# An attention and expert layer on one core: score units in pairs, triangles cleared by Pool, q and k split from the banks, first q sent in parts

## The chip, the cores and the metric

The kernel runs on one core of a Trainium2 chip. The metric is the device time of one execution in microseconds, lower is better. The core has TensorE (PE, its weight loads shown as PEld), VectorE (DVE), ScalarE (ACT), GpSimd (Pool) and SyncE (SP); SP, ACT and Pool issue the transfers.

## What is computed

The input has 4 batches of 512 tokens with 128 channels. Attention has 16 heads of 8 channels, a linear bias over the key position, and a causal mask; behind it stands a layer of 8 experts of which the best one's gate scales the sum of all outputs.

```python
q, k, v = (layernorm(x) @ w_attn + b_attn).reshape(b, t, 3, H, D).transpose(2, 0, 3, 1, 4)
scores = einsum('bhtd,bhsd->bhts', q, k) / sqrt(D) + slopes[None, :, None, None] * pos[None, None, None, :]
attn = softmax(where(causal, scores, -inf), axis=-1)
x = x + einsum('bhts,bhsd->bhtd', attn, v).transpose(0, 2, 1, 3).reshape(b, t, c) @ w_proj + b_proj
logits = layernorm(x) @ gate_w.T + gate_b            # normalised, softmax, top 1
h = gelu(einsum('nd,edh->neh', layernorm(x), w1) + b1)
out = x + ((einsum('neh,ehd->ned', h, w2) + b2) * norm_g[:, None, None]).sum(axis=1)
```

## The kernel before, in words

A batch b is worked in four sets s of four heads, so there are 16 sets, n = 4b + s. The scores are computed twice. First come 11 max units of a set (`max_unit`, L748): queries on the partitions, into one of three banks `v_ring`, and DVE takes row maxima of each 128-wide query block from there (L1099). PE transposes the maxima (`transpose_max`, L755), DVE splits them into m_hi and m_lo (L1115, L1116), and SP sends these into rows of `q_stack` (`load_max`, L398), so that the second computation of the scores subtracts them by itself. Its 12 score units (`exp_unit` on PE, L768 with the mask product L774) have keys on the partitions, go into three banks `a_ring`, and ACT takes the exponential into `probs` (L571). There are three kinds: four of kind 0 hold key block 0 with 512 query columns and one 128-wide triangle to mask, four of kind 1 hold blocks 1 and 3 (384 and 128 columns, two triangles), four of kind 2 hold block 2 (256 columns, one triangle). The triangles are masked by adding -1e30 with a bf16 product of identity and `score_mask`. `pv` (L793) multiplies probabilities and v, a kind at a time.

q and k of a batch are projected, DVE adds the bias (and scales q) into `q_full` and `k_full` (`take_q` L1056, `take_k` L1071), ACT copies the high part in a shorter format (`split_high`, L612), Pool subtracts it for the low part (`split_low`, L457; for the first q it is DVE, L1063), and SP, ACT and Pool send the parts into `q_stack` (L379, three transfers of 256 KB for all four sets) and `k_stack` (L335, 32 KB each).

Each engine's order is written out by hand: a set has 16 places, and the tables EARLY_PLAN (sets 0 to 4) and LATER_PLAN say at which place of set n the units of the next set's maxima (-1 means the end of the set before), `take_max` and the transposed maxima, the set's own score units and its `pv` stand. STAGES puts the side work of other batches there (the projections, norms, gates). The expert layer of batch b-1 fills sets from 5 on, and the last one's runs as a tail from about 268 us. On each engine at a place: side work, max units, take_max, score units, pv. Pool does norms (`z_rstd`, `x_rstd`, `norm_logits`), its part of k's sends, and `residual`, set by set. In the first set five max units of set 1 stand ahead of the first score unit.

## Time and profile before

| | |
|---|---|
| time, median of 3 runs (lowest to highest) | 317.34 us (316.98 to 338.38) |
| the profiled execution's own time | 317.27 us |
| its span | 315.5 us |
| PE busy | 292.7 us, 93% |
| DVE busy | 204.4 us, 65% |
| ACT busy | 193.5 us, 61% |
| Pool busy | 85.7 us, 27% |

The profile is of one execution. The span is the time from the first to the last recorded instruction. Matmuls are pipelined and their ends are modelled, so that a matmul's duration is longer than the distance to the next one. An idle time is put down to the instruction or transfer that released the engine.

### The profile page before, as it was taken

To read this page: it belongs to the slowest core of one execution; us is meant where nothing else is said; L and a number is where in the kernel's file an instruction comes from. 1 tells how busy PE (TensorE), PEld (TensorE's weight loads), DVE (VectorE), ACT (ScalarE), POOL (GpSimd) and SP (SyncE) were. 2 spreads that over 40 slices of the span, in tenths; PEclk is the share of its full clock that TensorE was granted. 3 is DMA by queue.
4 is the path that set the end of the run, shared out by engine and by line. 5 is a ranking of instruction groups with operands and counts; after the bars stand their busy time and mean duration, and the time that the engine had idled before them with its cause. 6 is when DMAs were issued, how large, how long until landed. Compare 5 with 4: busy or idle time off the path is not lost.

```text
span 315.5 us, 5489 instructions
## 1 busy us (share of the span) xinstructions
PE 292.7 (93%) x1750; PEld 184.2 (58%) x1751; DVE 204.4 (65%) x817; ACT 193.5 (61%) x323; POOL 85.7 (27%) x213
## 2 busy tenths in 40 slices
PE   7658698999969999999999999999999999999993
PEld 2524355666636666657666666657666665657871
DVE  5528589788877768554777785556776821266871
ACT  6462255557447478758667396857487877535462
POOL 3349411521133065002321172020300501600250
PEclk9795599999999999999999999999999999999999
DMA  6254400130400013002200132002001000000101
GB/s 173 105 150 126 137 2 0 35 124 6 108 12 0 0 38 127 3 0 59 63 3 2 34 89 76 0 21 66 0 6 35 2 2 2 0 0 1 35 0 33
DMA packets 12524, 13.23 MB, mean 42 GB/s; under 512 B 2064, under 2 KB 9104, under 8 KB 12240
## 3 DMA queue, kind: packets, MB, share of 16 engines
q1 hardware_dynamic: 11376, 11.70, 12.0%
q0 software_dynamic: 1024, 1.05, 1.6%
q8 instruction: 14, 0.23, 0.3%
q10 hardware_dynamic: 96, 0.13, 0.2%
q14 instruction: 14, 0.11, 0.1%
HBM read 5.14 MB, written 1.05 MB: 20 GB/s over the span
## 4 chain that ended last, share of the span: by engine, by line
PE 76%; DVE 10%; POOL 4%; DMA 3%; issue 2%; ACT 1%; SPq 1%; DVEq 0%; POOLq 0%; ACTq 0%
PE ffn_bank L861 14%; PE pv_bank L793 11%; PE a_ring L768 11%; PE v_ring L748 11%; PE a_ring L697 5%; PE a_ring L774 5%; PE a_ring L699 4%; PE a_ring L698 4%; DVE unused L1099 4%; DMA q_stack<-q_lo 1%; DMA q_stack<-m_lo 1%; PE v_ring L755 1%; PE v_ring L697 1%; PE v_ring L806 1%; PE v_ring L698 1%
## 5 line engine op out<-in xcount | busy, mean ns | idle before, releaser
L1099 DVE CUSTOM_DVE_ANT_0 unused<-v_ring,cst 128x256 bf16<-128x256 f32 (+3 forms) x256 | 112.2, 487 | 53.1 <-PE v_ring L748 49.3
L571 ACT ACTIVATE probs<-a_ring 128x512 f32<-128x512 f32 (+1 forms) x192 | 91.8, 526 | 62.3 <-PE a_ring L774 61.6
L748 PE MATMUL v_ring<-k_stack,q_stack 128*128 128x512 f32 (+1 forms) x176 | 84.1, 519 | 4.9 <-DMA q_stack<-q_lo 3.3
L768 PE MATMUL a_ring<-q_stack,k_stack 128*128 128x512 f32 (+3 forms) x256 | 73.5, 351 | 2.2 <-DMA q_stack<-m_lo 2.2
L588 ACT ACTIVATE hidden<-a_ring,cols_sb 128x512 f32<-128x512 f32 x64 | 43.4, 689 | 29.5 <-PE a_ring L699 29.2
L768 PEld LDWEIGHTS a_ring<-q_stack,k_stack 128*128 128x128 f32 x256 | 47.5, 195 | 14.9 <-issue 8.7
L861 PE MATMUL ffn_bank<-hidden,w_sb 128*128 128x512 f32 x100 | 51.9, 604 | 0.9 <-ACT hidden L588 0.9
L774 PE MATMUL a_ring<-score_mask,ident_bf 128*128 128x128 bf16 (+1 forms) x192 | 47.7, 250 | 0.0
L748 PEld LDWEIGHTS v_ring<-k_stack,q_stack 128*128 128x128 f32 x176 | 34.6, 205 | 21.6 <-issue 11.4
L793 PE MATMUL pv_bank<-probs,v_ones 128*32 128x256 f32 (+3 forms) x512 | 42.3, 440 | 0.0
L774 PEld LDWEIGHTS a_ring<-score_mask,ident_bf 128*128 128x128 bf16 x192 | 18.6, 97 | 25.4 <-issue 19.9
L335 POOL DMA_DIRECT2D k_stack<-k_lo x32 | 18.1, 569 | 54.3 <-PE a_ring L774 49.7
L697 PE MATMUL a_ring<-zT_hi,w_hi 128*128 128x512 f32 x64 | 28.2, 441 | 0.8 <-DVEq L998 0.8
L699 PE MATMUL a_ring<-zT_hi,w_lo 128*128 128x512 f32 x64 | 25.2, 394 | 0.0
L698 PE MATMUL a_ring<-zT_lo,w_hi 128*128 128x512 f32 x64 | 25.1, 392 | 0.0
L1099 DVE DVE_READ_ACCUMULATOR2_ANT row_max<- 128x1 f32 x256 | 21.3, 83 | 0.0
L861 PEld LDWEIGHTS ffn_bank<-hidden,w_sb 128*128 128x128 f32 x100 | 16.4, 193 | 3.8 <-ACT hidden L588 2.1
L793 PEld LDWEIGHTS pv_bank<-probs,v_ones 128*32 128x32 f32 x512 | 12.3, 109 | 10.7 <-issue 8.3
L697 PEld LDWEIGHTS a_ring<-zT_hi,w_hi 128*128 128x128 f32 x64 | 12.0, 188 | 9.1 <-issue 4.4
L588 ACT ACT_TABLE_LOAD x13 | 16.7, 1283 | 0.2
L571 ACT ACT_TABLE_LOAD x11 | 14.1, 1283 | 0.2
L341 POOL TENSOR_SCALAR var<-mv 128x4 f32<-128x4 f32 x6 | 1.1, 188 | 47.7 <-DVE mv L1006 47.7
(123 smaller groups left out, 346.5 us busy)
## 6 DMA issues: line engine op xcount, KB each, us to landing
q_stack<-q_hi SPq DMA_DIRECT2D x8, 256.0 KB
k_stack<-k_hi SPq DMA_DIRECT2D x60, 32.0 KB
x_in<-x SPq DMA_DIRECT2D x4, 256.0 KB, 3.4
hidden<-w SPq DMA_DIRECT2D x1, 1024.0 KB, 7.5
k_stack<-k_lo POOLq DMA_DIRECT2D x32, 32.0 KB, 2.1
q_stack<-q_lo SPq DMA_DIRECT2D x4, 256.0 KB
w_sb<-w SPq DMA_DIRECT2D x1, 1024.0 KB, 5.1
x_res<-x SPq DMA_DIRECT2D x4, 256.0 KB, 3.1
```

The source lines that it names most:

```text
L335: queue.dma_start(k_stack[ROW_Q * q + g::ROW_D, 2 * half:2 * half + 2, q, :].bitcast(F32), part[rows:rows + QR // 2, :].bitcast(F32)).then ...
L571: act.activation(probs[:, n % 2, q, KIND_AT[kind]:KIND_AT[kind] + cols], a_bank()[:, 0:cols], ACT.Exp).then_inc(e_freed, 1)
L588: act.activation(hidden[:, n % HB, :], a_bank()[:], ACT.Gelu, bias=b1_cols[:, m:m + 1]).then_inc(g_freed, 1)
L697: pe.matmul(dst, lhs[0], rhs[0], start=True, stop=False)
L698: pe.matmul(dst, lhs[0], rhs[1], start=False, stop=False)
L699: return pe.matmul(dst, lhs[1], rhs[0], start=False, stop=True)
L748: pe.matmul(dst, q_stack[b % 2][:, s, n * P:(n + 1) * P], k_stack[:, s, quads[0]:quads[-1] + 1, 0:cols], start=True, stop=True).then_inc(v ...
L768: pe.matmul(dst[:, at:at + P * (TB - j)], k_stack[:, s, q, j * P:(j + 1) * P], q_stack[b % 2][:, s, j * P:T], start=(at == 0), stop=False, ...
L774: pe.matmul(diagonal, ident_bf[:], score_mask[:].unsqueeze(1).to_broadcast([P, blocks, P]), start=False, stop=True, skip_group_check=True) ...
L793: last = pe.matmul(pv_bank[QR * q:QR * (q + 1), j * P:T], v_ones[b % 2][:, j, s, q, :], probs[:, n % 2, q, at:at + cols], start=(s % 2 == ...
L861: pe.matmul(ffn_bank[:], w2_sb[:, m, :], hidden[:, n % HB, :], start=(m == 0), stop=(m == NT - 1)).then_inc(ffn2_done, 1)
L1099: ins = dve.tensor_tensor_reduce(unused[:, (uses[0] - 1) % V_BANKS, at:at + cols], bank_[:, at:at + cols], cst[:, C_MASK + T - cols:C_MASK ...
```

## The change

- The four kind-2 units become two units of two heads each (two products of 256 columns, one mask product over two triangles, one exponential of 512 columns): a set has 10 score units.
- Kind 0 has no mask product. A constant row of the score product puts -1e30 on the corner of keys 64 to 127 against queries 0 to 63, and Pool clears the whole triangle of all four heads in `probs` with one `affine_select` on 128x4x128 per set (`mask_probs`), which waits for the set's fourth exponential; `pv` of kind 0 waits for it. On Pool it stands in front of `norm_logits` and `z_rstd`.
- DVE splits q and k itself from the projection's bank, two operations a part; ACT's copies, Pool's subtractions and `q_full`, `k_full` are gone. The scale of q is multiplied into w_attn and its bias by Pool at the start, and the split of w_attn moves behind `xn_ready` there.
- The corner's constant (256 KB) is loaded fourth. The first batch's q goes out in twelve transfers of 64 KB, set 0's three first. m_lo of the first set is sent by ACT. w_proj, w2 and the residual are loaded behind set 1's maxima.
- Set 0 has a plan of its own (FIRST_PLAN) with six max units of set 1 ahead of it and the transposed maxima at place 6; the exponentials' places in the other plans are fitted to 10 units.

```diff
-    "exp": (4, 4, 5, 6, 8, 8, 9, 11, 11, 13, 14, 14), "pv": (11, 15), "pv_last": (0,),
+    "exp": (4, 4, 5, 6, 8, 8, 9, 11, 12, 14), "pv": (11, 15), "pv_last": (0,),
+FIRST_PLAN = {
+    "max": (-1, -1, -1, -1, -1, -1, 0, 1, 2, 3, 4), "take_max": (6,),
+    "exp": (0, 1, 2, 3, 4, 5, 6, 7, 9, 10), "pv": (9, 12), "pv_last": (0,),
+}
...
-    "exp": (4, 5, 6, 7, 8, 9, 10, 10, 12, 13, 14, 15), "pv": (12, 15), "pv_last": (0,),
+    "exp": (4, 5, 6, 7, 8, 9, 10, 10, 13, 15), "pv": (12, 15), "pv_last": (0,),
...
+    KIND_UNITS = [[(0,), (1,), (2,), (3,)], [(0,), (1,), (2,), (3,)], [(0, 1), (2, 3)]]
+    EXP_UNITS = [(kind, quads) for kind in range(KINDS) for quads in KIND_UNITS[kind]]
+    KIND_END = [4, 8, 10]
...
+            def load_first_q(s, loaded):
+                sp.wait_ge(q_const, SETS)
+                for g, part in ((0, 0), (1, 0), (2, 1)):
+                    sp.wait_ge(q_split, part + 1)
+                    sp.dma_start(q_stack[0][g::ROW_Q, s, :].bitcast(F32),
+                                 (q_hi, q_lo)[part][s::SETS, :].bitcast(F32)).then_inc(loaded, 16)
...
+            sp.dma_start(corner, consts[:, C_CORNER:]).then_inc(corner_loaded, 16)
...
             load_k(0, 0, [0])
-            load_q(0)
+            load_first_q(0, first_q_loaded)
             load_k(0, 0, [3])
+            for s in range(1, SETS):
+                load_first_q(s, q_loaded)
             load_k(0, 1)
-            sp.dma_start(w_proj_sb[:], w_proj).then_inc(wp_loaded, 16)
-            sp.dma_start(w2_sb[:], w2).then_inc(w2_loaded, 16)
-            load_residual(0)
+            load_max(0, 0)
             load_x(1)
-            load_max(0, 0)
...
+            def mask_probs(n):
+                pool.wait_ge(e_freed, UNITS * n + KIND_END[0])
+                triangle = probs[:, n % 2, :, 0:P]
+                pool.affine_select(out=triangle, in_=triangle, compare_op=ALU.is_ge, fill=0.0, base=0,
+                                   pattern=[[0, QUADS], [1, P]], channel_multiplier=-1).then_inc(probs_masked, 1)
...
+            pool.wait_ge(rows_loaded, 32)
             pool.wait_ge(wa_loaded, 16)
+            pool.wait_ge(xn_ready, 1)
+            settle(pool.tensor_scalar(w_attn_sb[:, 0:C], w_attn_sb[:, 0:C], float(D) ** -0.5, None, ALU.mult))
             split(w_attn_sb[:], w_attn_hi[:], w_attn_lo[:], wa_split, 0)
-            pool.wait_ge(xn_ready, 1)
...
+                    if s == 2 and b + 1 < B:
+                        load_k_low(b + 1, 0)
+                    mask_probs(SETS * b + s)
+                    if s == 2 and b >= 1:
+                        norm_logits(b - 1)
+                    if s == 0 and b >= 1:
+                        z_rstd(b - 1)
...
+                kind, quads = EXP_UNITS[k]
...
+                for q in quads:
+                    for j in KEY_BLOCKS[kind]:
+                        last = pe.matmul(dst[:, at:at + P * (TB - j)], k_stack[:, s, q, j * P:(j + 1) * P],
+                                         q_stack[b % 2][:, s, j * P:T], start=(at == 0), stop=(kind == 0),
...
+                if kind == 0:
+                    last.then_inc(e_filled, 1)
+                    return
...
-                pe.wait_ge(e_freed, UNITS * n + QUADS * (kind + 1))
+                if kind == 0:
+                    pe.wait_ge(probs_masked, n + 1)
+                else:
+                    pe.wait_ge(e_freed, UNITS * n + KIND_END[kind])
...
+            def split_biased(src, bias, hi, lo, parts):
+                settle(dve.tensor_scalar(hi[:], src, bias, None, ALU.add))
+                dve.sem_inc(parts, 1)
+                settle(dve.scalar_tensor_tensor(out=lo[:], in0=src, scalar=bias, in1=hi[:].bitcast(F32),
+                                                op0=ALU.add, op1=ALU.subtract))
...
+        c[corner, C_KEY + HALF:C_KEY + P] = MASKED_SCORE
+        c[corner, C_CORNER:C_CORNER + HALF] = 1.0
```

The order of instructions on SP at the start, from the first sends of k on (k_hi, q_hi and q_lo are the split parts, m_hi the high part of the maxima; the shape is partitions by elements). Before:

```order
L335 DMA k_stack<-k_hi 8x2x512 [waits k_split,k_const]
L335 DMA k_stack<-k_hi 8x2x512
L379 DMA q_stack<-q_hi 32x4x512 [waits q_split,q_const]
L379 DMA q_stack<-q_hi 32x4x512 [waits q_split]
L379 DMA q_stack<-q_lo 32x4x512 [waits q_split]
L335 DMA k_stack<-k_hi 8x2x512 [waits k_split,k_const]
L335 DMA k_stack<-k_hi 8x2x512
L335 DMA k_stack<-k_hi 8x2x512 [waits k_split,k_const]
L335 DMA k_stack<-k_hi 8x2x512 x7
L416 DMA w_proj_sb<-w_proj 128x128
L417 DMA w_sb<-w 128x2048
L367 DMA x_res<-x 128x4x128
```

After, the same stretch's first rows; eight more k transfers, m_hi and the load of x follow behind these:

```order
L344 DMA k_stack<-k_hi 8x2x512 [waits k_split,k_const]
L344 DMA k_stack<-k_hi 8x2x512
L401 DMA q_stack<-q_hi 32x512 [waits q_split,q_const]
L401 DMA q_stack<-q_hi 32x512 [waits q_split]
L401 DMA q_stack<-q_lo 32x512 [waits q_split]
L344 DMA k_stack<-k_hi 8x2x512 [waits k_split,k_const]
L344 DMA k_stack<-k_hi 8x2x512
L401 DMA q_stack<-q_hi 32x512 [waits q_split,q_const]
L401 DMA q_stack<-q_hi 32x512 [waits q_split]
L401 DMA q_stack<-q_lo 32x512 [waits q_split]
L401 DMA q_stack<-q_hi 32x512 [waits q_split,q_const]
L401 DMA q_stack<-q_hi 32x512 [waits q_split]
```

The three q transfers have a quarter of their size, nine more stand between them and the rest of k.

On Pool in set 6, from k's sends of the next batch to the start of the logits' norm (its first operation is the one on `mean_square`). Before:

```order
L335 DMA k_stack<-k_lo 8x2x512 [waits k_split,e_filled]
L335 DMA k_stack<-k_lo 8x2x512 x3
L341 TENSOR_SCALAR var<-mean_square 128x4 [waits square_ready]
L342 TENSOR_SCALAR inverse_rms<-var 128x4 [waits pool_step]
L349 TENSOR_TENSOR var<-inverse_rms 128x4 [waits pool_step]
```

After:

```order
L344 DMA k_stack<-k_lo 8x2x512 [waits k_split,e_filled]
L344 DMA k_stack<-k_lo 8x2x512 x3
L512 AFFINE_SELECT probs<-probs 128x4x128 [waits e_freed]
L355 TENSOR_SCALAR var<-mean_square 128x4 [waits square_ready]
L356 TENSOR_SCALAR inverse_rms<-var 128x4 [waits pool_step]
L363 TENSOR_TENSOR var<-inverse_rms 128x4 [waits pool_step]
```

The select on `probs`, with its wait for ACT's exponentials, has come between the sends and the norm.

On PE in the first set, from the transposed maxima of set 0 (into `v_ring` from `row_max`) through the next set's max units to the first score units (into `a_ring`). Before:

```order
L755 MATMUL v_ring<-cst,row_max 16x128 [waits v_freed,max_ready]
L748 MATMUL v_ring<-k_stack,q_stack 128x512 [waits v_freed,q_loaded]
L748 MATMUL v_ring<-k_stack,q_stack 128x384 [waits v_freed]
L748 MATMUL v_ring<-k_stack,q_stack 128x512 [waits v_freed]
L748 MATMUL v_ring<-k_stack,q_stack 128x384 [waits v_freed]
L748 MATMUL v_ring<-k_stack,q_stack 128x512 [waits v_freed]
L768 MATMUL a_ring<-q_stack,k_stack 128x512 [waits m_loaded,mask_ready]
L774 MATMUL a_ring<-score_mask,ident_bf 128x128
L768 MATMUL a_ring<-q_stack,k_stack 128x512
L774 MATMUL a_ring<-score_mask,ident_bf 128x128
L748 MATMUL v_ring<-k_stack,q_stack 128x512 [waits v_freed]
```

After:

```order
L768 MATMUL v_ring<-cst,row_max 16x128 [waits v_freed,max_ready]
L761 MATMUL v_ring<-k_stack,q_stack 128x512 [waits v_freed,q_loaded]
L761 MATMUL v_ring<-k_stack,q_stack 128x384 [waits v_freed]
L761 MATMUL v_ring<-k_stack,q_stack 128x512 [waits v_freed]
L761 MATMUL v_ring<-k_stack,q_stack 128x384 [waits v_freed]
L761 MATMUL v_ring<-k_stack,q_stack 128x512 [waits v_freed] x2
L761 MATMUL v_ring<-k_stack,q_stack 128x384 [waits v_freed]
L783 MATMUL a_ring<-q_stack,k_stack 128x512 [waits m_loaded]
L761 MATMUL v_ring<-k_stack,q_stack 128x512 [waits v_freed]
L783 MATMUL a_ring<-q_stack,k_stack 128x512
L761 MATMUL v_ring<-k_stack,q_stack 128x384 [waits v_freed]
```

Two more max units stand ahead of the first score unit, and no mask product behind it.

## Rows read from the trace of the kernel before

**Rows 1.** The page, part 1: engine, busy us, share of the span, instructions.

```profile
PE 292.7 (93%) x1750; PEld 184.2 (58%) x1751; DVE 204.4 (65%) x817; ACT 193.5 (61%) x323; POOL 85.7 (27%) x213
```

**Rows 2.** Busy us by stretch: PE, PEld, DVE, ACT, POOL (count), PEclk, DMA share, GB/s.

```profile
36.00:45.00 9.00, 9.00 (x61) 5.46 (x60) 5.62 (x28) 5.88 (x12) 0.00 (x0) 0.82 0.01 2
45.00:60.00 15.00, 13.94 (x103) 8.62 (x103) 12.73 (x51) 6.71 (x14) 4.06 (x15) 1.00 0.02 6
...
120.00:200.00 80.00, 80.00 (x513) 51.34 (x512) 53.41 (x222) 56.41 (x95) 20.20 (x66) 1.00 0.14 43
```

**Rows 3.** Timeline of the start: start us, duration us, engine, line, operation, [idle before <-releaser].

```profile
6.28 1.00 POOL L446 TENSOR_TENSOR w_attn_lo<-w_attn_sb,w_attn_hi 128x384 fp32r<-128x384 f32 x1
...
13.44 0.75 DVE L1071 TENSOR_SCALAR k_full<-v_ring,cols_sb 128x512 f32<-128x512 f32 x1 [1.84 <-PE v_ring L699]
...
15.10 1.42 SPq L335 DMA_DIRECT2D k_stack<-k_hi  x2
...
16.62 1.24 SPq L379 DMA_DIRECT2D q_stack<-q_hi  x2
...
17.90 0.66 SPq L379 DMA_DIRECT2D q_stack<-q_lo  x1
...
22.28 1.51 PE L748 MATMUL v_ring<-k_stack,q_stack 128*128 128x512 f32 x3 [3.35 <-DMA q_stack<-q_lo]
...
31.19 0.68 SPq L398 DMA_DIRECT2D q_stack<-m_hi  x1
...
35.55 0.77 PE L768 MATMUL a_ring<-q_stack,k_stack 128*128 128x512 f32 x1 [2.23 <-DMA q_stack<-m_lo]
```

**Rows 4.** Timeline of set 7, first units, PE and DVE.

```profile
131.86 0.39 PE L768 MATMUL a_ring<-q_stack,k_stack 128*128 128x512 f32 x1
...
132.09 0.23 PE L774 MATMUL a_ring<-score_mask,ident_bf 128*128 128x128 bf16 x1
...
132.44 0.40 PE L768 MATMUL a_ring<-q_stack,k_stack 128*128 128x512 f32 x1
...
134.63 0.69 DVE L1099 CUSTOM_DVE_ANT_0 unused<-v_ring,cst 128x512 bf16<-128x512 f32 x1 [0.71 <-PE v_ring L748]
```

**Rows 5.** Timeline of sets 2 and 3 around the transposed maxima.

```profile
66.33 0.08 DVE L1099 DVE_READ_ACCUMULATOR2_ANT row_max<- 128x1 f32 x1
...
66.57 0.28 PE L755 MATMUL v_ring<-cst,row_max 128*16 128x128 f32 x1
...
76.42 0.36 PE L768 MATMUL a_ring<-q_stack,k_stack 128*128 128x256 f32 x1
...
76.67 0.36 PE L768 MATMUL a_ring<-q_stack,k_stack 128*128 128x256 f32 x1
```

**Rows 6.** The groups by line and shape: busy us, mean ns of one | idle before.

```profile
L457 POOL TENSOR_TENSOR k_lo<-k_full,k_hi 128x512 fp32r<-128x512 f32 x4 | 5.1, 1280 | 31.4 <-ACT k_hi L612 31.4
...
L507 POOL TENSOR_SCALAR_AFFINE_SELECT score_mask<-zeros 128x128 bf16<-128x128 f32 x1 | 0.3, 289 | 0.0
```

**Rows 7.** Timeline of set 6: Pool, ACT, PE and DVE.

```profile
118.14 0.18 POOL L341 TENSOR_SCALAR var<-mean_square 128x4 f32<-128x4 f32 x1 [0.18 <-DVE mean_square L1164]
...
118.44 4.60 ACT L571 ACTIVATE probs<-a_ring 128x512 f32<-128x512 f32 x9 [0.22 <-PE a_ring L774]
...
122.35 1.06 PE L793 MATMUL pv_bank<-probs,v_ones 128*32 128x512 f32 x8
...
122.59 1.28 POOL L526 TENSOR_TENSOR xb_res<-x_res,rows_sb 128x512 f32<-128x512 f32 x1
...
123.35 0.19 DVE L1169 TENSOR_REDUCE rt<-lg 128x4 f32<-128x32 f32 x1
```

**Rows 8.** Timeline of sets 0 and 1: the last maxima's send and the first score unit.

```profile
44.48 0.62 SPq L398 DMA_DIRECT2D q_stack<-m_lo  x1
...
46.71 0.40 PE L768 MATMUL a_ring<-q_stack,k_stack 128*128 128x512 f32 x1
```

**Rows 9.** Timeline of set 8: DVE behind Pool's rstd.

```profile
158.35 1.12 DVE L1012 TENSOR_SCALAR z<-x,mv,rstd 128x128 f32<-128x128 f32 x4 [0.23 <-POOLq L491]
```

More of the change, by code:

```diff
@@ L41 @@
 MASKED_SCORE = -1.0e30
+HALF = P // 2
 EPS_LN = 1e-5
@@ L336, in send_k, with send_max @@
                             part[rows:rows + QR // 2, :].bitcast(F32)).then_inc(loaded, 16)
+        def send_max(queue, row, part, b, s):
+            queue.dma_start(q_stack[b % 2][row:row + ROW_D - CONST_TERM:ROW_Q, s, :].bitcast(F32),
+                            part[:].bitcast(F32)).then_inc(m_loaded, 16)
         def inverse_sqrt(engine, settle, y, src, scale, eps, v, t, fused=False):
@@ L396, in load_max @@
                 sp.wait_ge(m_ready, SETS * b + s + 1)
-                for r, part in ((MAX_ROWS, m_hi), (MAX_ROWS + ROW_D, m_lo)):
-                    sp.dma_start(q_stack[b % 2][r:r + ROW_D - CONST_TERM:ROW_Q, s, :].bitcast(F32),
-                                 part[:].bitcast(F32)).then_inc(m_loaded, 16)
+                send_max(sp, MAX_ROWS, m_hi, b, s)
+                if (b, s) != (0, 0):
+                    send_max(sp, MAX_ROWS + ROW_D, m_lo, b, s)
             def store(b):
@@ L446, in split @@
                 pool.tensor_tensor(lo, src, hi.bitcast(F32), ALU.subtract).then_inc(done, 1)
-            def split_low(b, part):
-                full, hi, lo, parts, loads, count = (
-                    (k_full, k_hi, k_lo, k_split, k_low_loaded[0] + k_low_loaded[1], K_LOW_LOADS * b),
-                    (q_full, q_hi, q_lo, q_split, [q_loaded], q_count(b)))[part]
-                pool.wait_ge(parts, 2 * b + 1)
-                if b >= 1:
-                    for loaded in loads:
-                        pool.wait_ge(loaded, count)
-                pool.tensor_tensor(lo[:], full[:], hi[:].bitcast(F32), ALU.subtract).then_inc(parts, 1)
             def set_ones(tile, e):
@@ L601, in gate_exponentials @@
                 act.activation(lge[:], lg2[:], ACT.Exp, scale=2.0).then_inc(gate_exp, 1)
-            def split_high(b, part):
-                full, hi, ready, parts, loads, count = (
-                    (k_full, k_hi, k_ready, k_split, k_loaded[0] + k_loaded[1], K_LOADS * b),
-                    (q_full, q_hi, q_ready, q_split, [q_loaded], q_count(b)))[part]
-                act.wait_ge(ready, b + 1)
-                if b >= 1:
-                    for loaded in loads:
-                        act.wait_ge(loaded, count)
-                act.activation(hi[:], full[:], ACT.Copy).then_inc(parts, 1)
             def q_constants(i):
                 for s in range(SETS):
-                    act.activation(q_stack[i][:, s, :], zeros[:], ACT.Identity,
+                    act.activation(q_stack[i][:, s, :], corner, ACT.Identity,
                                    bias=cst[:, C_QUERY + s:C_QUERY + s + 1]).then_inc(q_const, 1)
@@ L759, in exp_unit @@
                 n = SETS * b + s
-                kind, q = k // QUADS, k % QUADS
-                if n == 0 and k == 0:
+                kind, quads = EXP_UNITS[k]
+                if n == 0 and kind == 1:
                     pe.wait_ge(mask_ready, 2)
```

110 lines of the change are left out of this document (50 added, 60 removed).

## The prediction

> **What bounds the kernel now.** I read the page's busy shares first, then the busy time by stretches, then the timeline at the start and in single sets. The page has PE busy for 93% of the span [rows 1]. By stretches the reader is to see three regimes [rows 2]: from 36 to 45 us PE is busy all the time while its granted clock averages 0.82 (it is at the half level, 1.2 GHz, at first and then at 2.4 GHz); from 45 to 60 us DVE is busy 12.7 of 15 us; from 120 to 200 us PE is busy all 80 us at full clock, with DVE at 53. A busy PE is a modelled figure, so I looked for what it waits for. In every set the row maxima of the next set end on DVE, and PE then transposes them (L755). In set 2 the last readout ends at 66.41 and the transpose starts at 66.57 [rows 5]: PE and DVE come together there, so PE work taken away ahead of that point is only worth something where DVE has idle time. In sets 2 and 3 DVE's maxima run without a pause. In set 7, with feed-forward work in between, DVE idles for 0.71 us in front of one maximum because PE is late [rows 4]; there PE bounds.
>
> Before 36 us neither bounds. The first scores' row maxima wait for a chain: k from its bank at 13.44, SP's sends from 15.10, the last q part issued at 17.90, first maximum on PE at 22.28, maxima sent at 31.19, first score unit at 35.55 after an idle of 2.23 us put down to m_lo's landing [rows 3].
>
> The sum is made against the profiled run's own 317.27 us (span 315.5 and 1.8 around it), 0.07 under the median of 317.34.
>
> **Part 1: the start.** Before, k_hi was a copy of ACT behind DVE's 0.75 us addition [rows 3]; now DVE's own operation at 13.44 leaves k_hi at 14.19, so SP can issue at about 14.3 instead of 15.10. Folding the scale into the weights puts Pool's split of them (its subtraction alone 1.00 us [rows 3]) behind the normalised x; about 1.7 us of Pool work there ends close to when the projection starts anyway, and I put that and the 256 KB corner load at 0, at worst +0.5. q_lo ends after four DVE operations of 0.75, at 16.4, so the first set's three q transfers are out by 17. The first q is a quarter as long. From the issue at 17.90 to the first maximum were 4.4 us behind 0.75 MB; with 0.19 MB I take 2.7 (bounds 2.2, the lone landing below, and 4.4), so the maxima start near 19.6 and m can be sent 8.9 us later (22.28 to 31.19), at 28.5.
>
> By then SP is not free: ahead of m_hi it now issues 2 + 3 + 2 + 9 + 8 = 24 transfers. At 0.62 to 0.71 us each (1.24 for two, 1.42 for two [rows 3]) they take 14.9 to 17.0; with 0.64, from 14.3, to 29.7. A lone m transfer is used 2.23 us after its issue (44.48 to 46.71 [rows 8]), and m_lo goes out on ACT beside it, while the loads that shared the queues go later. First score unit at 31.9: **-3.6**, bounds -1.5 (0.71 per issue, and 0.5 late) and -4.1 (0.62).
>
> The Trainium skill, "DMA: Bandwidth & Descriptors", Rules for kernel authors, advises against this part: small transfers should be coalesced, since below 64 KB one pays mostly overhead; each q transfer is now 64 KB. By the Trainium skill's table there (0.95 us busy for 64 KB, 6.15 for 1 MB), an estimate for the twelve q transfers is 11.4 us of transfer against 4.6 for the three large ones (a quarter of the 1 MB each), and were the difference on the path the sum would be +1.9 instead of -4.9. The rows rather show the issue pace on SP as the limit, which the sum has.
>
> **Part 2: set 0.** It took 11.16 us from first score unit to set 1's (35.55 to 46.71 [rows 3, 8]), PE busy throughout. The clock of 0.82 over 36 to 45 means half level for 0.36 x 9 = 3.2 us, to 39.2; so 3.65 us of the stretch at half and 7.5 at full are 9.3 us of work at full clock. Out of it go four masks at about 0.13 (below), 0.24 for the pairs and two more max units that stand ahead of the first score (seven instead of five), 0.23 each: 1.2 in all. As much of it stays at half clock I take 10.1 us: **-1.1**, bounds 0 (if the early units' banks hold PE up, DVE being the slower) and -2.
>
> **Part 3: q and k of the next batch.** ACT's copies and Pool's subtractions (1.28 us each [rows 6]) were off PE's path; now DVE does two operations of 0.75 per part instead of one, 1.5 us more in sets 1, 5 and 9. In set 1 DVE is nearly the bound (12.7 of 15 us [rows 2]): **+0.9**, between 0 and +1.5. In 5 and 9 idle time takes some of it, counted below. Removing work from ACT is put at 0: ACT had slack; and Pool's freed 2.6 us hide nothing.
>
> **Part 4: masks and pairs on PE.** In set 7 an unmasked step of 512 columns is 0.23 (131.86 to 132.09) but unit, mask and max unit together take 0.58 (131.86 to 132.44 [rows 4]); 0.58 - 2 x 0.23 = 0.12 to 0.13 for a mask with its weight load. A third-kind unit with mask is 0.25 (76.42 to 76.67 [rows 5]); a pair is 2 x 0.12 + 0.13 = 0.37, so 0.12 saved per pair. On PE this is 64 x 0.13 + 32 x 0.12 = 12.1 us over the kernel. Little of it arrives. The third kind's saving is made up by order: one such unit stood ahead of L755 and both pairs stand behind it, so what is saved comes back as a wait for DVE. The first kind's 0.52 per set counts only where DVE pauses. By sets: 1 to 4, 8 and 12 nothing (DVE, or the layer norm of part 5); 7, 11 and 13 -0.5 each; 5 and 9 -0.5 each, after DVE's added work; 15 -0.3, since ACT's exponentials are near; 14 +0.1. That is -2.7. ACT's exponential of a pair is one of 512 columns instead of two of 256, a gain of some 0.17 off the path.
>
> **Part 5: Pool's select.** 16 instructions on 128x512. No row has that form. From below: 0.289 us, the select of 128x128 [rows 6]; from above 1.28, Pool's two-input operation on 128x512 (and 4 x 0.289 = 1.16). I take 0.6, as the operation has one input and the fixed part comes once. The Trainium skill, "GPSIMD Engine Reference", Elementwise, has 769 ns for a 512-element operation of the simplest kind; with it sets 6 and 10 would lose 0.2 us more each. The select starts when the fourth exponential is freed; the product with v that needs it comes after the second kind's units, in set 6 at 122.35 [rows 7], some 1.3 us of slack beyond 120.7 and a fast select. What stands behind it on Pool matters. In set 6 the logits' norm ran on Pool from 118.14 until the residual's start at 122.59, DVE's gating took it up at 123.35, between the maxima and the m operations [rows 7]. Now the select stands ahead of it, and it waits for the fourth of ACT's exponentials that begin at 118.44, about 120.7 (nine take 4.60); with 0.6 the norm starts at 121.2 and ends at 125.6, 3 us later, DVE's route and m 2.3 us later. PE's second max unit of set 8 then waits for a bank, about 0.9 us: **+0.8** each in sets 6 and 10 (0 to +1.5). In sets 4, 8 and 12 the same holds for the second norm's rstd (158.35 on DVE waits for Pool [rows 9]); a few tenths late, which cancels part 4 there.
>
> **Sum.** -3.6 - 1.1 + 0.9 - 2.7 + 1.6 = -4.9, so 317.3 - 4.9 = **312.4 us**. The bounds together are about -10 and +1.
>
> **Rivals.** *PE's savings all count where DVE has any pause* (the orders rearrange themselves and Pool's delay lies under feed-forward work): parts 1 to 3 -3.8, 0.76 in eleven sets, 0.4 each in sets 6 and 10: -9.2 more, 304.3. For it: 80 of 80 us busy on PE; against it: the transpose that waits for DVE. *SP's queue eats the start*: at 0.71 per issue and a q landing no faster than 4.4 us, the first score comes at 34, set 0 gains half and the DVE work of set 1 costs its full 1.5: -1.5 - 0.5 + 1.5 - 1.1 = -1.6, 315.7. For it: 24 issues instead of 19 ahead of m_hi; against: k goes out 0.8 us earlier, and only the first three q transfers are needed early. The Trainium skill's rule on small transfers, named above, is this rival. *The other side: Pool's select is slow.* The select stands in front of the product in 16 sets with some 1.3 us of slack; at 2.4 us it costs 1.1 in each and 1.8 more in sets 6 and 10 and in the three with rstd: 17.6 + 9 - 4.9, 339. It outweighs the gains from about 1.4 us per select, and is slower by 2% from about 1.7. The Pool rows of this size lie below that.
>
> **How the numbers follow.** About 2%, 6.3 us, is what a measurement of this kernel can tell from no change: faster is under 311.0, slower over 323.7. The forecast and its neighbourhood (311 to 315) 0.45; the first rival and values between it and the forecast 0.37; the queue 0.12; the slow select 0.06, four fifths of it over the bound. So faster 0.37, same 0.58, slower 0.05. The range takes the first rival nearly whole and the queue: 305 to 316.5; the forecast's own is 310.5 to 315.
>
> **What would show it.** In the profile of the changed kernel: SP's m_hi issue near 29.7 directly behind k's transfers, first score unit at 31.9, set 1's at 42.1; the transposed maxima still right behind DVE's last readout; the select at 0.6 us; Pool's norm in set 6 ending 3 us behind its place before, with PE pausing at the second max unit. Wrong would be: m ready after SP is free; PE savings that pass the transpose; a select over 1.3 us; or a stall at the product with v.

## The result

The changed kernel took 320.30 us (median of 9 runs, 318.22 to 323.33) where the kernel before took 317.34: a ratio of 1.0083, 95% interval 1.0063 to 1.0104. It is slower by 0.8%, outside the forecast range of 305 to 316.5 and on the other side of no change than its centre of 312.4. It stays within 2%, which the prediction held likeliest, but that is no merit of its sum, which pointed the other way. Without one slow run of each kernel (338.38 before, 323.33 after), which the ratio leaves out, the times run from 316.35 to 318.59 before and from 318.22 to 322.44 after; this scatter is taken up again below.

The profiled run of the changed kernel has a span of 318.7 us, 3.2 more than before. The first part of its page, beside [rows 1], and the select's row among its costliest groups (busy us, mean ns of one, idle before and what ended it):

```profile
PE 290.1 (91%) x1654; PEld 184.9 (58%) x1655; DVE 210.6 (66%) x824; ACT 183.8 (58%) x283; POOL 87.3 (27%) x224
...
L512 POOL TENSOR_SCALAR_AFFINE_SELECT probs<-probs 128x512 f32<-128x512 f32 x16 | 10.1, 631 | 108.0 <-ACT probs L595 108.0
```

PE has 96 instructions less, ACT 10 us less to do, and the select takes 0.63 us, estimated at 0.6. So the work went away, and the time did not follow. Where it went can be read by cutting the trace at the first score unit of each set. The lengths below, each from one profiled run, are differences of those starts, for the kernel before, the changed one, and six of the experiments told further down (us; "first" is the first score unit of set 0, the last row the end of the span):

| stretch | before | changed | changed minus before | forecast | e1 | e3 | e4 | e8b | e11 | e9 |
|---|---|---|---|---|---|---|---|---|---|---|
| to first | 35.55 | 33.22 | -2.33 | -3.6 | 33.29 | 32.85 | 33.32 | 34.79 | 32.50 | 30.36 |
| set 0 | 11.15 | 11.36 | +0.21 | -1.1 | 10.10 | 10.10 | 10.09 | 11.78 | 10.77 | 10.55 |
| set 1 | 14.44 | 16.08 | +1.64 | +0.9 | 16.09 | 15.94 | 14.37 | 14.81 | 16.09 | 14.37 |
| set 5 | 17.95 | 17.59 | -0.36 | -0.5 | 17.61 | 17.61 | 17.30 | 17.41 | 17.59 | 17.25 |
| set 6 | 13.93 | 17.12 | +3.19 | +0.8 | 13.58 | 14.84 | 15.57 | 15.51 | 15.55 | 13.57 |
| set 7 | 17.07 | 16.57 | -0.50 | -0.5 | 16.56 | 16.56 | 16.56 | 16.54 | 16.54 | 16.54 |
| set 8 | 18.36 | 18.68 | +0.32 | 0 | 18.72 | 18.76 | 18.72 | 18.50 | 18.74 | 18.70 |
| set 9 | 18.41 | 18.96 | +0.55 | -0.5 | 18.97 | 18.97 | 18.04 | 17.87 | 18.95 | 18.05 |
| set 10 | 13.93 | 15.52 | +1.59 | +0.8 | 13.57 | 14.82 | 17.13 | 15.51 | 15.55 | 13.59 |
| set 11 | 17.07 | 16.55 | -0.52 | -0.5 | 16.56 | 16.56 | 16.56 | 16.54 | 16.55 | 16.54 |
| set 14 | 12.31 | 12.78 | +0.47 | +0.1 | 11.90 | 12.48 | 12.81 | 12.80 | 12.80 | 11.85 |
| end | 315.45 | 318.71 | +3.26 | -4.9 | 312.22 | 314.76 | 316.33 | 315.63 | 315.86 | 306.50 |

Of the sets left out of the table, 2 to 4 gained at most 0.14, set 12 lost 0.44, set 13 gained 0.46, and set 15 with the tail gained 0.70. Six stretches carry most of the error of 8.2 us: sets 6 and 10 together 3.2 us worse than forecast, the start 1.3, set 0 another 1.3, sets 1 and 9 together 1.8.

The largest, set 6, from the timeline of the changed kernel (start, duration, engine, line, operation, idle before and its releaser; the rows answer to [rows 7]):

```profile
119.38 0.63 POOL L512 TENSOR_SCALAR_AFFINE_SELECT probs<-probs 128x512 f32<-128x512 f32 x1 [4.67 <-ACT probs L595]
...
120.65 1.07 PE L817 MATMUL pv_bank<-probs,v_ones 128*32 128x512 f32 x8
...
121.80 0.28 PE L768 MATMUL v_ring<-cst,row_max 128*16 128x128 f32 x1
...
124.18 0.50 PE L761 MATMUL v_ring<-k_stack,q_stack 128*128 128x512 f32 x1
...
124.42 1.26 POOL L550 TENSOR_TENSOR xb_res<-x_res,rows_sb 128x512 f32<-128x512 f32 x1
124.49 0.19 DVE L1189 TENSOR_REDUCE rt<-lg 128x4 f32<-128x32 f32 x1 [2.80 <-POOL lg L520]
124.71 1.01 DVE L1190 TENSOR_TENSOR lg<-lg,rt 128x32 f32<-128x32 f32 x1
125.65 0.27 DVE L1135 TENSOR_SCALAR m_hi<-v_ring 16x128 fp32r<-16x128 f32 x1
125.95 0.28 DVE L1136 SCALAR_TENSOR_TENSOR m_lo<-v_ring,m_hi 16x128 fp32r<-16x128 f32 x1
...
126.35 0.44 PE L761 MATMUL v_ring<-k_stack,q_stack 128*128 128x384 f32 x1 [1.67 <-DVEq L1138]
```

and the same places of the kernel before:

```profile
123.57 0.34 DVE L1170 TENSOR_TENSOR lg<-lg,rt 128x32 f32<-128x32 f32 x1
...
124.14 0.28 DVE L1116 SCALAR_TENSOR_TENSOR m_lo<-v_ring,m_hi 16x128 fp32r<-16x128 f32 x1
...
125.62 0.68 PE L748 MATMUL v_ring<-k_stack,q_stack 128*128 128x512 f32 x2
```

Pool idles for 4.67 us until the fourth exponential lets it begin the select, and the norm, which in the kernel before began 0.21 us into the set, stands behind it. The select is done at 120.01, and PE takes its result at 120.65 without a wait. DVE sits for 2.80 us in front of its routing step while the transposed maxima lie in their bank (the product ends at 122.08). So m_lo ends at 126.23, and PE, which asked for that bank right behind its product at 124.18, waits 1.67 us. Counted from the set's first score unit (116.80, before 117.93), PE is at that product 0.31 us earlier than before, because masks and pairs had gone; the wait takes that back and more. The routing step begins 2.27 us later than before, which is what was forecast (2.3). m_lo ends 2.94 us later: the other 0.67 is L1190, 1.01 us where L1170 took 0.34. It ends at 125.72, right behind Pool's residual (125.68), which stands directly behind the norm on Pool.

What happens behind the wait stands in the busy time by stretches (columns as in [rows 2]):

```profile
36.00:45.00 9.00, 9.00 (x61) 5.36 (x59) 5.51 (x29) 4.24 (x8) 3.39 (x15) 0.82 0.35 97
119.00:127.00 8.00, 6.25 (x57) 3.50 (x56) 4.74 (x22) 4.74 (x8) 5.07 (x18) 1.00 0.27 99
127.00:136.00 9.00, 9.00 (x36) 6.41 (x29) 4.51 (x17) 5.69 (x9) 0.00 (x0) 0.81 0.01 2
...
128.00:131.50 3.50, 3.50 (x10) 2.69 (x9) 0.76 (x4) 1.99 (x3) 0.00 (x0) 0.51 0.01 2
...
195.00:206.00 11.00, 9.33 (x55) 6.10 (x44) 6.68 (x22) 7.44 (x12) 1.85 (x4) 1.00 0.01 4
```

From 127 to 136 us the granted clock is 0.81: PE worked at the half level (1.2 GHz) for 2 x 0.19 x 9 = 3.4 us. This stretch lies between 128 and 131.5 us and begins less than 2 us behind the wait, in which PE was idle for 1.67 us in one piece. At full level that work takes 1.7 us less. The same wait in set 10 (inside 195 to 206) left the clock at 1.00, and this set lost 1.59 us instead of 3.19. So a wait of this length is followed by the fall in some places and runs and not in others.

The fall is not the changed kernel's alone. Every run has a PE wait of 1.5 to 1.6 us in set 4. In e4, e5 and e10 (the last is the kernel before with one number altered) the half level follows it, and set 4 takes 20.4 to 20.5 us; in the kernel before and in the other runs it does not, and set 4 takes 18.8 or 18.9. The stretch behind that wait in e10, then in the kernel before:

```profile
92.00:96.00 4.00, 4.00 (x30) 2.08 (x29) 3.52 (x14) 0.00 (x0) 0.78 (x4) 0.57 0.02 4
...
92.50:97.00 4.50, 4.48 (x39) 3.04 (x40) 3.40 (x13) 1.24 (x3) 0.51 (x3) 1.00 0.02 5
```

### The profile page after: what moved, and what is told of

Its sections match the earlier page's. It is cut to its first block, busy times and chain, and to the rows that moved or that the text cites. A ratio compares the mean times of both kernels' runs of the same rounds, so it can differ in the third digit from the quotient of the medians.

```text
span 318.7 us, 5265 instructions
## 1 busy us (share of the span) xinstructions
PE 290.1 (91%) x1654; PEld 184.9 (58%) x1655; DVE 210.6 (66%) x824; ACT 183.8 (58%) x283; POOL 87.3 (27%) x224
## 3 DMA queue, kind: packets, MB, share of 16 engines
q0 software_dynamic: 1024, 1.05, 1.6%
HBM read 5.40 MB, written 1.05 MB: 20 GB/s over the span
## 4 chain that ended last, share of the span: by engine, by line
PE 53%; DVE 18%; POOL 9%; issue 6%; ACT 5%; DMA 3%; SPq 3%; ACTq 1%; DVEq 0%; POOLq 0%
PE ffn_bank L885 11%; DVE unused L1119 9%; PE a_ring L783 7%; PE v_ring L761 7%; PE pv_bank L817 6%; PE a_ring L708 5%; PE a_ring L709 4%; PE a_ring L710 4%; DMA rows_sb<-rows 2%; PE a_ring L795 2%; ACT probs L595 2%; POOL var L364 2%; SPq L344 2%; POOL var L365 1%; POOL var L363 1%
## 5 line engine op out<-in xcount | busy, mean ns | idle before, releaser
L595 ACT ACTIVATE probs<-a_ring 128x512 f32<-128x512 f32 x160 | 87.2, 600 | 78.7 <-PE a_ring L795 53.7
L783 PE MATMUL a_ring<-q_stack,k_stack 128*128 128x512 f32 (+3 forms) x256 | 64.9, 335 | 1.0 <-DMA q_stack<-m_hi 0.7
L783 PEld LDWEIGHTS a_ring<-q_stack,k_stack 128*128 128x128 f32 x256 | 46.1, 197 | 14.9 <-issue 5.0
L512 POOL TENSOR_SCALAR_AFFINE_SELECT probs<-probs 128x512 f32<-128x512 f32 x16 | 10.1, 631 | 108.0 <-ACT probs L595 108.0
L708 PE MATMUL a_ring<-zT_hi,w_hi 128*128 128x512 f32 x64 | 28.9, 452 | 0.8 <-DVEq L1022 0.8
L795 PE MATMUL a_ring<-score_mask,ident_bf 128*128 128x256 bf16 x96 | 27.6, 288 | 0.0
L709 PE MATMUL a_ring<-zT_lo,w_hi 128*128 128x512 f32 x64 | 25.8, 404 | 0.0
L710 PEld LDWEIGHTS a_ring<-zT_hi,w_lo 128*128 128x128 f32 x64 | 12.5, 195 | 2.9
```

Of the source, the lines that this page charges most:

```text
L595: act.activation(probs[:, n % 2, quads[0]:quads[-1] + 1, KIND_AT[kind]:KIND_AT[kind] + cols], a_bank()[:, 0:len(quads) * cols].rearrange(" ...
L708: pe.matmul(dst, lhs[0], rhs[0], start=True, stop=False)
L709: pe.matmul(dst, lhs[0], rhs[1], start=False, stop=False)
L710: return pe.matmul(dst, lhs[1], rhs[0], start=False, stop=True)
L783: last = pe.matmul(dst[:, at:at + P * (TB - j)], k_stack[:, s, q, j * P:(j + 1) * P], q_stack[b % 2][:, s, j * P:T], start=(at == 0), stop ...
L795: pe.matmul(diagonal, ident_bf[:], score_mask[:].unsqueeze(1).to_broadcast([P, blocks, P]), start=False, stop=True, skip_group_check=True) ...
```

## The experiments

The theories: **A**, Pool's select pushes the norm back, DVE's routing step waits for it in front of the m operations, and PE waits for their bank; **C**, the clock at the start takes back what the start gains; further ones come with the runs, and some expectations give the letter A to the cause that they test.

**e1: the routing step behind take_max**

```diff
-    "z_norm": (0, 13, 1), "z": (0, 15, 1), "logits": (2, 4, 1), "route": (2, 13, 1), "gates": (3, 13, 1),
+    "z_norm": (0, 13, 1), "z": (0, 15, 1), "logits": (2, 4, 1), "route": (2, 14, 1), "gates": (3, 13, 1),
```

> The changed kernel with one number altered: DVE's routing step (its first operation is L1189) stands at place 14 behind take_max instead of place 13 ahead of it. Theory A (the select delays Pool's norm, DVE waits for the norm in front of the m operations, PE waits 1.67 us for their bank in sets 6 and 10, and the clock falls behind such a wait): both PE gaps go, set 6 falls from 17.8 us to about 13.1 and set 10 from 16.2 to about 13.1, granted clock 1.00 in 127 to 136 us, 320.3 - 4.7 - 3.1 = 312.5 us. Theory B (what costs is the longer way to the logits themselves or the select's presence, the place of the routing does not matter): 319 to 321 us.

314.87 us, ratio 0.9907 (0.9873 to 0.9942): 5.4 us under the changed kernel, by one number in a table, and 2.4 over the 312.5 expected. (The expectation starts from lengths of 17.8 and 16.2 us for sets 6 and 10, where the table above has 17.12 and 15.52, so it put the gain too high.) Its timeline in set 6:

```profile
120.66 0.28 PE L768 MATMUL v_ring<-cst,row_max 128*16 128x128 f32 x1
...
120.97 0.28 DVE L1135 TENSOR_SCALAR m_hi<-v_ring 16x128 fp32r<-16x128 f32 x1 [0.43 <-PE v_ring L768]
...
123.03 0.68 PE L761 MATMUL v_ring<-k_stack,q_stack 128*128 128x512 f32 x2
...
123.38 0.19 DVE L1189 TENSOR_REDUCE rt<-lg 128x4 f32<-128x32 f32 x1 [0.75 <-POOL lg L520]
```

The m operations follow the transposed maxima at once, the two max units come in one group without a wait between them, and the routing still waits for Pool, now in front of nothing. Sets 6, 10 and 14 go from 17.12, 15.52 and 12.78 to 13.58, 13.57 and 11.90, each 0.35 to 0.4 under the kernel before. Set 15 with the tail gave 0.9 us of it back (57.05 against 56.14); why was not tried. Theory A holds; B (the place does not matter) falls.

**e10: the same number in the kernel before.** The edit is that of e1.

> The kernel before with the routing step at place 14 and nothing else. Theory A (the place only matters where the norm comes late): 317 to 317.5 us, sets 6 and 10 unchanged within 0.2. Rival (the place is a gain of its own that the changed kernel could not have lost): under 316 us.

317.50 us, ratio 1.0008 (0.9993 to 1.0024), sets 6 and 10 at 13.93 each, as in the kernel before. The place of the routing was free as long as the norm came early; the change made it matter.

**e3: the norm ahead of the select**

```diff
-                    mask_probs(SETS * b + s)
                     if s == 2 and b >= 1:
                         norm_logits(b - 1)
+                    mask_probs(SETS * b + s)
```

> The changed kernel with the logits' norm on Pool ahead of the select in sets 6, 10 and 14, as it stood before the change; the select then comes behind 4.5 us of norm. Theory A: the wait for the bank in front of the second max unit goes, but PE's product with v in these sets now waits for the select, which ends near 122.8 in set 6 instead of 120.0, some 2.1 us behind the place where PE asks for it (120.65); sets 6 and 10 about as long as now, 319 to 321.5 us. Theory B (the norm's place alone costs): 315 to 316 us.

316.81 us, ratio 0.9982 (0.9961 to 1.0004), between the two theories' ranges (319 to 321.5 and 315 to 316). The wait only changes its place: in set 6 PE's product with v now waits for Pool.

```profile
119.66 0.64 POOL L512 TENSOR_SCALAR_AFFINE_SELECT probs<-probs 128x512 f32<-128x512 f32 x1
...
120.35 1.06 PE L817 MATMUL pv_bank<-probs,v_ones 128*32 128x512 f32 x8 [1.35 <-POOL probs L512]
```

It is 1.35 us, where 2.1 was expected: the norm began at 115.22, ahead of the first exponential at 115.52, and was done at 119.71. Sets 6 and 10 take 14.84 and 14.82, 0.9 over before, and neither shows a fall of the clock. Select and norm in one queue cost something in either order as long as somebody waits for the second.

**e11: PE kept at work in the wait**

```diff
+            def fill_wait(b, s, count):
+                n = len(a_uses)
+                pe.wait_ge(*a_uses[n - A_BANKS])
+                for _ in range(count):
+                    pe.matmul(a_ring[n % A_BANKS][:], k_stack[:, s, 0, 0:P], q_stack[b % 2][:, s, :],
+                              start=True, stop=True)
...
             def max_unit(b, s, k):
+                if k == 1 and b >= 2 and s == 0:
+                    fill_wait(b - 1, 2, 7)
```

> The changed kernel with seven spare products of 512 columns (1.6 us of work whose results are thrown away) in the place where PE waits for the bank in sets 6 and 10; nothing else moves. Theory E (besides the wait itself the clock's fall behind it costs about 1.6 us in the sets and runs where it comes): sets 6 and 10 both about 15.6 us, full clock throughout 119 to 136 and 195 to 206, 318.2 us with the runs closer together. Rival (only the wait costs, the clock falls for other reasons): 320.3 us or more.

317.89 us, ratio 1.0015 (1.0002 to 1.0028): 2.4 us less than the changed kernel, by adding products that nobody reads. Sets 6 and 10 are both 15.55, and the clock stays up in both places:

```profile
127.00:136.00 9.00, 9.00 (x41) 6.54 (x40) 5.16 (x22) 7.97 (x14) 0.64 (x1) 1.00 0.00 1
195.00:206.00 11.00, 11.00 (x55) 7.77 (x56) 6.83 (x25) 8.18 (x14) 0.64 (x1) 1.00 0.01 4
```

So in set 6 the 3.19 us split into 1.6 for the wait (15.55 - 13.93) and 1.6 for the clock behind it (17.12 - 15.55). In e4, whose order in these sets is that of the changed kernel, it was set 10 that had the fall (17.13) and set 6 that had not (15.57). One profile with the clock up proves little, as e8b has it up behind such waits too, but the mean granted clock of every run is on record: 0.962 (0.954 to 0.969, nine runs) in the changed kernel and 0.970 (0.965 to 0.976, twelve runs) in e11, whose start is the same. The difference is worth some 2.4 us of 318, the whole gain. The times are closer together too (316.81 to 319.27), and theory E holds. The scatter of the changed kernel goes with the same figure: its fastest run, 318.22, has 0.969, its slowest, 323.33, has 0.955. The falls behind other waits (set 4) and the half level's length at the start are in this figure as well.

**e4: q and k of later batches split by ACT and Pool again** (the first batch stays with DVE)

```diff
-    "gates": (3, 1, 1),
+    "k_high": (1, 7, -1), "q_high": (1, 9, -1), "gates": (3, 1, 1),
...
                     mask_probs(SETS * b + s)
+                    if s == 1 and b + 1 < B:
+                        split_low(b + 1, 0)
+                        split_low(b + 1, 1)
...
-                split_biased(bank_[:], bk, k_hi, k_lo, k_split)
+                    split_biased(bank_[:], bk, k_hi, k_lo, k_split)
+                    return
+                dve.wait_ge(k_split, 2 * b)
+                settle(dve.tensor_scalar(k_full[:], bank_[:], bk, None, ALU.add))
...
```

> The changed kernel in which for batches 1 to 3 ACT copies the high part of q and k and Pool subtracts, as before the change (DVE one operation a part); the first batch stays with DVE. Theory A (DVE's 1.5 us more work in sets 1, 5 and 9 is on the path in set 1 and partly in 9): set 1 falls from 16.1 to about 14.9 us, set 9 by about 0.5, 318.7 us. Rival (it is hidden, what costs in set 1 is something else): 320 us.

316.38 us, ratio 0.9950 (0.9915 to 0.9985), 3.9 us less. Sets 1, 5 and 9 are 1.71, 0.29 and 0.92 us shorter than in the changed kernel, 2.9 together and more than expected; the rest of the 3.9 lies within the scatter of both (313.75 to 319.72 here). The reason stands in set 1 of the changed kernel:

```profile
53.09 0.75 DVE L1076 TENSOR_SCALAR k_hi<-v_ring,cols_sb 128x512 fp32r<-128x512 f32 x1 [0.15 <-DVE row_max L1119]
...
54.00 0.75 DVE L1078 SCALAR_TENSOR_TENSOR k_lo<-v_ring,cols_sb,k_hi 128x512 fp32r<-128x512 f32 x1 [0.16 <-DVE k_hi L1076]
...
55.07 0.28 DVE L1135 TENSOR_SCALAR m_hi<-v_ring 16x128 fp32r<-16x128 f32 x1 [0.32 <-PE v_ring L710]
```

One more operation of 0.75 with 0.16 of settling stands in front of m_hi, and another one behind it in front of the next set's maxima. On ACT and Pool the same work was hidden: set 1 is back at 14.37 (14.44 before).

**e2: the first m_hi ahead of eight k transfers**

```diff
-            load_k(0, 1)
             load_max(0, 0)
+            load_k(0, 1)
```

> The changed kernel with SP's send of the first m_hi ahead of the eight k transfers for sets 2 and 3 instead of behind them. Theory A (SP's issue order sets the first score unit): m_hi goes out at 29.4 instead of 31.4 us, the first score unit starts at 31.3 instead of 33.2, and the end moves by -1.9, to 318.4. Theory C (the clock's rise near 39.3 us takes the start's gain back, since PE works at half level until then whatever it starts with): first score unit at 31.3 but set 1's first unit moves by less than 1 us, end 319.5 to 320.3.

320.03 us, ratio 1.0058 (1.0024 to 1.0093). The first score unit starts at 31.78, 1.44 earlier, but the median moves by 0.3 only. Set 1's first unit came 2.36 us earlier (42.22 against 44.58), where C had less than 1; but the half level also ended earlier in this run, so that is not all the send's doing. Behind it sets 6 and 10 both had the clock's fall (17.14, 17.13), and set 2 took 10.91 instead of 9.69. Which of the theories holds can't be said from it.

**e5: e1 and e2 together**

> The changed kernel with both the routing step at place 14 and SP's first m_hi ahead of the eight k transfers. With no PE gap in sets 6 and 10 the clock disturbs the comparison less. Theory A (SP's order is worth 1.4 us at the first score unit and it lasts): 314.9 - 1.4 = 313.5 us. Theory C (set 0 then only runs longer at the half clock): 314.5 to 315 us.

313.31 us, ratio 0.9863 (0.9844 to 0.9882), first score unit at 31.43. Against e1 that is 1.6 us less, as theory A has it; the two intervals overlap a little. In the profiled runs set 1's first unit came at 41.93 against 43.39 in e1, so 1.46 us of the start's gain were still there; the spans are equal (312.2) because e5's run had a fall of the clock in set 4 and e1's had not. This speaks for A. That the gain was covered in e2 by the falls of the clock fits its sets 2 and 10, and was not tried by itself.

**e6: e5 and e4 together**

> The kernel of both edits and, besides, ACT's and Pool's splits of q and k for batches 1 to 3. If the three causes add (routing 5.4, split 2.9 by the sets' lengths, first m_hi up to 1.4 us): 311 us, 2% under the kernel before, sets 1, 6, 9 and 10 near 14.4, 13.5, 18.0 and 13.5 us. If they share one wait, 313 to 314.5 us.

309.68 us, ratio 0.9763 (0.9740 to 0.9787). The causes add up: it is 1.3 us under the 311 expected. With e4's whole 3.9 us and e5's 1.6 in place of the 2.9 and 1.4, the sum is 320.3 - 5.4 - 3.9 - 1.6 = 309.4. In the profiled run, which at 311.14 is one of the longer ones, the first score unit came only at 33.09: Pool began its scaling at 10.75 there, behind the rows' load (9.91 in the changed kernel, 9.76 in e5). That wait is what e9 takes away.

**e9: e6, and Pool scales w_attn without waiting for the rows of constants**

```diff
-            pool.wait_ge(rows_loaded, 32)
             pool.wait_ge(wa_loaded, 16)
...
+            pool.wait_ge(rows_loaded, 32)
             pool.tensor_scalar(bq, bq, float(D) ** -0.5, None, ALU.mult).then_inc(bias_scaled, 1)
```

> The kernel of routing, first m_hi and splits, in which Pool's scaling of w_attn no longer stands behind its wait for the rows of constants (the wait moves to the bias, which needs them). Theory D (Pool idled until 9.9 to 10.8 us for that load and the projection came 0.5 to 1.3 us later than before the change): the scaling starts at about 8.6, the projection at 10.9 to 11.2 instead of 12.3 to 13.1, the first score unit 1.2 to 2 us earlier, 308.3 us. Rival (the clock at the start gives it back): 309.5 us.

308.11 us, ratio 0.9703 (0.9689 to 0.9718), 1.6 us less than e6 and clear of its interval: D holds, and the rival (309.5) falls. The start of the changed kernel, where the rows answer to [rows 3]:

```profile
9.91 0.55 POOL L534 TENSOR_SCALAR w_attn_sb<-w_attn_sb 128x128 f32<-128x128 f32 x1 [7.58 <-DMA rows_sb<-rows]
...
12.26 0.77 PE L708 MATMUL v_ring<-xT_hi,w_attn_hi 128*128 128x512 f32 x1 [2.44 <-POOL w_attn_lo L472]
...
14.82 1.50 SPq L344 DMA_DIRECT2D k_stack<-k_hi  x2
...
31.39 0.68 SPq L349 DMA_DIRECT2D q_stack<-m_hi  x1
...
33.22 0.80 PE L783 MATMUL a_ring<-q_stack,k_stack 128*128 128x512 f32 x1 [0.70 <-DMA q_stack<-m_hi]
```

and in e9:

```profile
8.72 0.56 POOL L548 TENSOR_SCALAR w_attn_sb<-w_attn_sb 128x128 f32<-128x128 f32 x1 [6.37 <-DVE xn L1069]
...
11.09 0.47 PE L741 MATMUL v_ring<-xT_hi,w_attn_hi 128*128 128x512 f32 x1 [1.17 <-POOL w_attn_lo L476]
...
30.36 0.63 PE L816 MATMUL a_ring<-q_stack,k_stack 128*128 128x512 f32 x1
```

In the changed kernel the scaling stood behind a load that it does not use, and the projection came 1.2 us later than in e9. (The first score unit of e9 is also earlier because m_hi goes out ahead of eight k transfers, as in e2.)

**e12: e9 without the plan of its own for set 0**

```diff
-            return FIRST_PLAN if n == 0 else EARLY_PLAN if n <= SETS else LATER_PLAN
+            return EARLY_PLAN if n <= SETS else LATER_PLAN
```

> The kernel with routing, first m_hi, splits and the rows' wait moved, but with the first set on the plan of the other early sets (four max units of set 1 ahead of its first score unit and one more at its place 4, the transposed maxima at place 12) instead of its own. Theory F (the plan of set 0 with its six early units is worth the two max units moved out of the set and the earlier send of the maxima, 0.5 to 1.0 us): 308.6 to 309.1 us, set 0 longer by that. Rival (PE is bound by what it has to do at the half clock anyway): 308.1 us, within 0.3.

307.50 us, ratio 0.9689 (0.9662 to 0.9715), no different from e9 within the intervals; set 0 takes 10.50 against 10.55. The six early units are worth nothing that can be measured. This version and e9 beat both kernels, by 3% of the time before.

**e7: pairs alone, on the kernel before.** The units of after's exp_unit and its places, with all masks on PE.

> The kernel before with the pairs of third-kind units alone (10 units a set, pairs at places 12 and 14 or 13 and 15, all masks on PE). Theory A (the pair's saving is given back as a wait at the transposed maxima): 316.5 to 317.5 us, sets 7, 11 and 13 shorter by 0.2 at most. Rival (every PE saving counts, 32 x 0.12 = 3.8 us): 313.5 us.

317.83 us, ratio 1.0006 (0.9990 to 1.0023). Sets 6, 7, 10 and 11 are 13.97, 17.08, 13.96 and 17.08, and no set gained more than 0.12: the pairs brought nothing, as the prediction had said. In these four sets the transposed maxima start 0.68 us behind the start of the PE instruction ahead of them, 0.52 before: 0.16 of the saving is given back there, where PE waits for DVE's last readout. Where the rest went was not followed.

**e8b: triangles alone, on the kernel before.** No mask product for kind 0, the corner's constant and load, and on Pool the changed kernel's order:

```diff
+                    if s == 2 and b + 1 < B:
+                        load_k_low(b + 1, 0)
+                    mask_probs(SETS * b + s)
...
+                    if s == 2 and b >= 1:
+                        norm_logits(b - 1)
+                    if s == 0 and b >= 1:
+                        z_rstd(b - 1)
...
```

> The kernel before with Pool's select for the first kind alone: no mask product there, the corner's constant loaded fourth, the select ahead of the norm on Pool, routing at place 13. Theory A: sets 7, 11 and 13 gain 0.5 us each, sets 6 and 10 lose 1.5 to 2 each by PE's wait for the bank behind the delayed routing and 1.5 more where the clock falls behind it: 317 to 320 us. Rival (the select costs nothing, 64 masks count): 309 to 313 us.

318.07 us, ratio 1.0018 (1.0005 to 1.0030). Sets 5, 7, 9 and 11 gain 0.5 each; sets 6 and 10 lose 1.58 each, as much as set 10 of the changed kernel, with the clock up in both. So the wait there is wholly the doing of the select in front of the norm.

## Why the prediction was wrong

The step that failed by most is the price of the wait in sets 6 and 10: 0.8 us each was forecast, 3.19 and 1.59 were measured (part 5). The terms of the start, set 0 and DVE's extra work were too favourable by 1.3, 1.3 and 1.8 us. None of the signs of being wrong that the prediction named came: m was ready before SP was free, sets 2 to 4 gained next to nothing, the select took 0.63, and PE did not stall at the product with v. The pause at the second max unit came as forecast, only longer.

**Part 1, the start**: the mechanism (SP's queue up to m_hi) was right, the term was -3.6 and measured -2.33. Two steps of its sum were mis-sized. One was put at "0, at worst +0.5": Pool's scaling waited for the rows until 9.91, so k went out at 14.82 instead of 14.3 (0.5). The other is the pace: SP needed 16.6 us for 24 transfers instead of 15.4 (1.2; 0.4 of it was a wait for the first q part), inside the bounds that the prediction gave. The use of m_hi 1.83 us after its issue instead of 2.23 gave 0.4 back. m was ready by 29.2, before SP, as forecast.

**Part 2, set 0**: -1.1 was forecast and +0.21 measured in the profiled run, but -1.05 in e1, whose instructions up to set 5 are the same. In the changed kernel's run the clock from 36 to 45 is 0.82 as before, though PE had started 2.3 us earlier, so that the half level covered 6.1 us of the set instead of 3.65. In e1 the clock of that stretch is 1.00. The changed kernel's set 0 up to 39.3, then e1's row:

```profile
33.20:39.30 6.10, 6.08 (x20) 5.02 (x20) 3.88 (x20) 3.74 (x7) 1.41 (x4) 0.50 0.14 43
...
36.00:45.00 9.00, 8.38 (x63) 4.52 (x62) 6.26 (x35) 4.91 (x11) 3.41 (x15) 1.00 0.42 145
```

I had taken the half level's part of the stretch from one run as if it belonged to the kernel. The work itself fell about as forecast: 6.1 us at half and 5.3 at full level are 8.3 us at full clock, where 9.3 - 1.2 = 8.1 was forecast. (With 3.65 us at half that makes 9.9 and not the 10.1 of the prediction.) The plan's part of the term is nothing by e12; what the masks' part is was not tried by itself.

**Part 3, q and k**: right in kind, too small. +0.9 in set 1 was 1.71 by e4, a little over the upper bound of 1.5, and in set 9 the 0.92 of DVE's extra work turned the forecast -0.5 into +0.55.

**Part 4, masks and pairs**: right. Sets 7, 11 and 13 gained 0.50, 0.52 and 0.46 where 0.5 was forecast, the pairs alone nothing, sets 2 to 4 at most 0.14 each. Set 15 with the tail gained 0.70 where 0.3 was forecast.

**Part 5, the select**: its price (0.6 forecast, 0.63 measured) and the mechanism were right; the size of the loss, +0.8 each in sets 6 and 10, was the failing term. The routing step came 2.27 us later in the set, as forecast with 2.3. But Pool's residual came later with the norm and fell on DVE's second routing operation, which then took 0.67 us more (below); without the clock's fall the set lost 1.59, and these 0.67 are most of what it lost beyond 0.8. The clock's fall, 1.6 us in set 6 of the profiled run, was not in the sum or in a rival at all. Together 4.8 instead of 1.6. In set 14 the same delay of the routing, put at +0.1 with the masks, cost 0.47, and e1 took 0.88 off it. In sets 8 and 12 the change lost 0.32 and 0.44 where the forecast had gain and delay cancel; triangles alone (e8b) lost 0.14 and 0.16 there, pairs alone (e7) 0.08 and 0.20, and the cause was not tried by itself.

Of the rivals, the queue (315.7) had two of the right pieces: a later first score unit (34 there, 33.22 measured) and DVE's work in set 1 at its full 1.5. The slow select was priced on the wrong cause: a select of 0.63 us is enough where it stands in front of somebody else's wait. The Trainium skill, "DMA: Bandwidth & Descriptors", Rules for kernel authors, advises against small transfers, and the prediction's estimate by the table of that page made the start 6.8 us worse than -3.6, so later than before. The first score unit came 2.33 us earlier, so that size did not come; no run tried twelve transfers against three by themselves.

## What to carry to other kernels

When work is put into an in-order queue, price what stands behind it on that queue, then what stands behind the waiter of that, and look which operations of two engines will fall on each other when a queue shifts. A wait that costs a microsecond or two on TensorE can cost as much again through the clock behind it; filling it or moving the waiter by one place is worth trying before the work is undone. A start that is bound by one queue's issues is paid in the order of that queue and in the waits of the engines that feed it, so look at every wait there for loads that the instruction does not use.
